# New orders for every engine of a LayerNorm, selective scan and int8 matmul kernel, from tables of place numbers

## The reference, cut to what matters

```python
def reference(x, A_log, D, x_proj_w, dt_proj_w, dt_proj_b, weight_q, weight_scale, bias):
    x = x + s6(layernorm(x), A_log, D, x_proj_w, dt_proj_w, dt_proj_b)
    x = x + quantized_ffn(layernorm(x), weight_q, weight_scale, bias)
    return x                                       # x is (8, 2048, 512) f32

def s6(x, ...):                                    # 512 features d, 16 states n
    xp = einsum('bld,ed->ble', x, x_proj_w)        # 64 ranks, 16 of B, 16 of C
    delta = softplus(xp[..., :64] @ dt_proj_w.T + dt_proj_b)
    h = exp(delta * -exp(A_log)) * h_before + delta * B * x    # for each row l in turn
    return sum over n of h * C + x * D

def quantized_ffn(x, ...):                         # 512 to 512
    x_scale = max(max(abs(x)), 1e-6) / 127.0       # of each row
    x_q = int8(clip(round(x / x_scale), -128, 127))
    return int32(x_q @ weight_q.T) * x_scale * weight_scale + bias
```

## Time and profile before

| | |
|---|---|
| median of 3 runs | 2763.84 us (2761.54 to 2764.33) |
| the profiled execution, first to last instruction | 2760.5 us |
| busy: PE, DVE, ACT, POOL | 2736.5, 2705.4, 2690.0, 2691.9 us |
| DVE: 2048 scans | 1828.9 + 584.8 us |
| POOL: 511 products by C | 2342.0 us |
| moved by DMA | 344.35 MB |

### The profile page before, as it was taken

The page is one execution under the profiler, slowest core; times in us unless marked ns, Lnnn a source line. Parts: engine busy times, 40 slices in busy tenths (PEclk is TensorE's granted clock), DMA queues, the critical chain, the costliest instruction groups (busy, mean ns, idle before and its releaser), DMA issues.

```text
span 2760.5 us, 59331 instructions
## 1 busy us (share of the span) xinstructions
PE 2736.5 (99%) x22612; PEld 2519.7 (91%) x22612; DVE 2705.4 (98%) x2801; ACT 2690.0 (97%) x4927; POOL 2691.9 (98%) x981
## 2 busy tenths in 40 slices
...
GB/s 198 100 101 139 123 116 148 107 124 133 118 142 117 120 142 123 116 143 112 124 131 116 145 112 117 149 112 127 137 118 124 127 117 149 111 113 154 99 133 54
DMA packets 271654, 344.35 MB, mean 125 GB/s; under 512 B 174917, under 2 KB 174917, under 8 KB 251018
## 3 DMA queue, kind: packets, MB, share of 16 engines
...
HBM read 253.60 MB, written 103.16 MB: 129 GB/s over the span
## 4 chain that ended last, share of the span: by engine, by line
PE 97%; DVE 1%; ACT 1%; issue 0%; DMA 0%; SPq 0%; DVEq 0%; POOL 0%; ACTq 0%
PE Y L855 32%; PE PB L830 23%; PE PB L833 21%; PE Y L851 4%; PE PM L962 4%; PE PM L921 4%; PE PM L902 4%; PE PM L892 2%; PE PM L930 2%; DVE A L994 1%; PE PM L909 0%; ACT A L669 0%; ACT DB L688 0%; PE PM L872 0%; PE PM L879 0%
## 5 line engine op out<-in xcount | busy, mean ns | idle before, releaser
L604 POOL TENSOR_TENSOR A<-A,CB 128x2048 f32<-128x2048 f32 x511 | 2342.0, 4747 | 42.4 <-ACT CAR L676 40.9
L994 DVE TENSOR_TENSOR_SCAN A<-A,CAR,PB 128x512 f32<-128x512 f32 x1536 | 1828.9, 1260 | 9.9 <-ACT A L669 4.6
L669 ACT ACTIVATE A<-DEL,an 128x512 f32<-128x512 f32 x2048 | 1332.5, 713 | 6.3 <-PE Y L855 5.8
L855 PE MATMUL Y<-idf,A 128*128 128x128 f32 x8192 | 1085.1, 273 | 0.0
L855 PEld LDWEIGHTS Y<-idf,A 128*128 128x128 f32 x8192 | 932.7, 141 | 6.5 <-issue 0.5
L688 ACT ACTIVATE DB<-XN,BC 128x512 f32<-128x512 f32 x1344 | 891.7, 711 | 3.6 <-DVE XN L1024 3.6
L833 PE MATMUL PB<-idf,DB 128*128 128x128 f32 x5376 | 764.1, 273 | 8.4 <-DVE A L994 7.0
L830 PEld LDWEIGHTS PB<-DG,XN 128*128 128x128 f32 x5632 | 685.9, 192 | 70.8 <-issue 48.3
L830 PE MATMUL PB<-DG,XN 128*128 128x128 f32 x5632 | 726.7, 276 | 2.5 <-DVE A L994 2.4
L833 PEld LDWEIGHTS PB<-idf,DB 128*128 128x128 f32 x5376 | 621.7, 141 | 66.3 <-issue 39.5
L994 DVE TENSOR_TENSOR_SCAN A<-A,PB 128x512 f32<-128x512 f32 x512 | 584.8, 1201 | 12.5 <-PE PB L833 7.4
...
## 6 DMA issues: line engine op xcount, KB each, us to landing
CB<-c_rows SPq DMA_DIRECT2D x128, 1024.0 KB, 4.8
DG<-b_diag SPq DMA_DIRECT2D x192, 256.0 KB, 5.0
X<-in_x SPq DMA_DIRECT2D x31, 1024.0 KB, 7.3
out<-X SPq DMA_DIRECT2D x31, 1024.0 KB, 5.2
out<-bias_rows POOLq DMA_DIRECT2D x31, 1024.0 KB, 8.8
out<-C POOLq DMA_DIRECT2D x31, 1024.0 KB, 12.7
...
b_diag<-BC SPq DMA_DIRECT2D x192, 2.0 KB, 5.4
```

The costliest lines, as they stand in the source:

```text
L604: gp.tensor_tensor(A[s % NA][:, :, :], A[s % NA][:, :, :], CB[:, s % (4 * NG), :].unsqueeze(1).broadcast_to([128, KB, L]), ALU.mult).then_ ...
L669: act.activation(A[s % NA][:, g, :], DEL[k % 2][:, g, :], ACT.Exp, scale=an[:, g, n:n + 1])\
L855: i = pe.matmul(Y[j][:, g * 128:(g + 1) * 128], A[s % NA][:, g, j * 128:(j + 1) * 128], idf[:, :], is_transpose=True, start=False, stop=(n ...
L994: dve.tensor_tensor_scan(A[s % NA][:, g, :], A[s % NA][:, g, :], PB[(4 * s + g) % NPB][:, :], init, ALU.mult, ALU.add).then_inc(s_scan, 1)
```

## The change

PERIOD goes from 1000 to 10000, and every number of PLACES, FIRST and LAST is replaced. No instruction is added to or removed from a chunk, and waits, tiles and sizes stay. The code below the tables is the same, 17 lines further down (L441 is L458 afterwards, L994 is L1011). Of the tables, two lines of PLACES:

```diff
-PERIOD = 1000
+PERIOD = 10000
 PLACES = {
...
-        "load_c": (107, 189, 717, 1001),
+        "load_c": (-1828, 3705, 4565, 6870),
...
-        "put_x": (1260,),
+        "put_x": (8967,),
```

More of the change, by code:

```diff
@@ L3 @@
 from contextlib import ExitStack
-PERIOD = 1000
+PERIOD = 10000
 PLACES = {
[L8 to L36, removed]
-        "load_c": (107, 189, 717, 1001),
-        "load_g": (35, 113, 310, 426, 1034, 1035),
-        "log0": (-1321,),
-        "put_last": (30000, 30001, 30002, 30003),
-        "put_x": (1260,),
[L42 to L60, removed]
[8 rows of a table removed]
[L69 to L80, removed]
@@ new lines @@
+        "act_b": (-2204, -2091, -2081, -2007, -1997, -1964, -1236, -1212, -1196, -470, -210, -161, -131, 203,
+        235, 278, 302, 464, 930, 1115, 1544, 2000, 2045, 2130, 2227, 2272, 2428, 2654, 2665, 3261, 3303, 4751,
+        5680, 5742, 5791, 5924, 6032, 6161, 6418, 6463, 6673, 6799),
+        "add_b": (19628,),
+        "add_c": (21943,),
+        "aggr0": (-11131,),
+        "amax": (14650,),
+        "ascale": (14042,),
+        "b_c": (-4324,),
+        "bc_out": (-5011,),
+        "bias_p": (200000, 200001, 200002, 200003),
@@ new lines @@
+        "idle": (200000, 200001, 200002, 200003),
+        "inv": (14968,),
+        "last_p": (200000, 200001),
+        "last_q": (200000, 200001, 200002, 200003),
+        "last_v": (200000, 200001),
+        "late": (200000, 200001, 200002, 200003),
+        "load": (-17500,),
+        "load_c": (-1828, 3705, 4565, 6870),
+        "load_g": (-4271, -3355, -1713, -192, 3547, 5496),
+        "log0": (-13308,),
+        "put_last": (200000, 200001, 200002, 200003),
+        "put_x": (8967,),
+        "q_mm": (18557, 18884, 20116, 20799),
@@ new lines @@
+        "q_t": (200000, 200001, 200002, 200003),
+        "qt_out": (17992, 19529, 20193, 23955),
+        "root": (14490,),
+        "rstd0": (-12916,),
+        "scale_a": (18084, 18731, 19205, 19848),
+        "scale_out": (200000, 200001, 200002, 200003),
+        "scale_p": (20893,),
+        "scales": (15617,),
+        "scan": (677, 897, 908, 931, 1340, 1345, 1345, 1345, 1345, 1345, 1353, 1353, 1548, 1608, 2429, 2586,
[4 rows of a table added]
+        "square": (13603, 13726, 14091, 14201),
+        "stats0": (-16595, -14243, -13892, -13758),
@@ new lines @@
+        "step": (15112,),
+        "store_c": (-2091,),
+        "store_g": (-4344,),
[8 rows of a table added]
+        "times_c": (252, 2574, 2845, 3650, 3931, 3936, 3942, 3981, 4386, 5182, 6947, 7062, 9064, 9717, 9807,
+        9949),
+        "turn": (17150,),
+        "var1": (14440,),
+        "warm": (200000, 200001, 200002, 200003, 200004, 200005, 200006, 200007, 200008, 200009, 200010,
+        200011),
+        "weights": (200000, 200001),
+        "x_p": (-5085, -5015, -4961, -4800),
+        "x_t": (-7595, -7130, -6858, -5430),
@@ L104 @@
[L104 to L125, removed]
@@ new lines @@
+        4074, 4082, 4164, 4301, 4827, 5313, 5348, 5399, 5662, 5683),
+        "add_b": (13976,),
+        "add_c": (22755,),
+        "aggr0": (-56395,),
+        "amax": (14678,),
+        "ascale": (14015,),
+        "b_c": (-58841,),
+        "bc_out": (-47619,),
+        "carry": (-361, 51, 421, 1952, 2030, 3180, 3468, 4394, 5109, 5368, 6433, 6555, 6971, 7088, 7908, 9360),
+        "centre": (15018, 15018, 15021, 16423),
+        "d_t": (-58762, -58091, -57284, -56741),
+        "decay": (-1680, -1458, -1424, -1406, -1404, -1404, -1404, -1404, -1404, -1394, -1391, -1304, -643,
[3 rows of a table added]
@@ new lines @@
+        "delta": (-46238, -38371, -37853, -36878),
+        "dl_t": (-50668, -49981, -43372, -41835),
+        "du": (-50897, -49054, -48113, -44153),
+        "gather": (11594, 12196, 12536, 12727),
+        "inv": (14875,),
+        "late": (-56500, -56400, 1000, 2000),
+        "load_c": (-56900, 3705, 4565, 6870),
+        "load_g": (-56800, -56700, -56600, -56300, 3547, 5496),
+        "log0": (-67199,),
+        "put_x": (14352,),
+        "q_mm": (18561, 18830, 19510, 20688),
+        "qt_out": (17846, 19083, 21458, 24188),
@@ new lines @@
+        "root": (14592,),
+        "rstd0": (-64776,),
+        "scale_a": (18302, 18701, 19418, 19751),
+        "scale_p": (21528,),
+        "scales": (15442,),
+        "scan": (699, 717, 717, 717, 717, 717, 721, 1043, 1043, 1059, 1101, 1188, 1724, 2210, 2371, 2442, 2582,
[4 rows of a table added]
+        "square": (12575, 13320, 13365, 13490),
+        "stats0": (-66507, -64549, -62297, -59886),
+        "step": (14395,),
+        "store_c": (-66375,),
+        "store_g": (-63242,),
[8 rows of a table added]
+        "times_c": (3601, 5384, 5547, 5683, 5829, 6218, 6767, 6942, 7433, 8752, 9636, 9832, 9844, 9844, 9984,
@@ L155 @@
+        10047),
+        "turn": (16687,),
+        "var1": (13568,),
+        "warm": (-50669, -50669, -1032, -1032, -1032, -1032, -1032, -1032, -1032, -1032, -1032, -1032),
+        "weights": (-659, 8151),
+        "x_p": (-63112, -59532, -59176, -59076),
+        "x_t": (-69956, -69193, -67385, -64745),
+        "xn": (-62645, -58697, -57917),
+        "xn_p": (-52454,),
+        "xp_out": (-54175,),
+        "xt_d": (-52727, -51805),
+        "xt_out": (-57532, -57272, -57272, -56808),
 }
@@ new lines @@
+        "aggr0": (-10553,),
+        "amax": (12118,),
+        "ascale": (12082,),
+        "b_c": (-4488,),
+        "bc_out": (-5434,),
+        "bias_p": (12332, 12336, 13115, 13540),
+        "carry": (-695, 434, 758, 1123, 2248, 2905, 3113, 4072, 5217, 5665, 6979, 7186, 7365, 7933, 8070, 8841),
+        "d_t": (-4062, -3929, -3802, -3548),
+        "decay": (-1977, -1790, -1490, -1146, -926, -811, -628, -619, -618, -614, -600, -153, 196, 233, 340,
[3 rows of a table added]
+        "delta": (-4588, -4478, -4209, -3682),
```

122 lines of the change are left out of this document (52 added, 70 removed), and 74 rows, old and new, of tables (FIRST, LAST, PLACES).

## The result

The changed kernel takes 2887.49 us (2886.3 to 2890.61, 4 runs) against 2763.45 (2761.54 to 2764.33, 4 runs): ratio 1.0452, 95% interval 1.0437 to 1.0466. That is 124 us more; forecast were 102 more, 2866 us, with a range to 2900.

What follows compares the result with a forecast made beforehand. PE, DVE, ACT and POOL in lockstep were taken as the bound, with DVE nearly full in three chunks of four. Steady chunks +98, opening +3 and end +1 gave +102, so 2866 us; range 2760 to 2900, likeliest case 2825 to 2900.

Steps and rivals of the forecast that it cites:

- L: Time from the end of the fourth gather until group 1 of CB has landed: 16.8 us, bounds 15 and 17.8.
- the share of `add_c`: What SP's queue loses to POOL's `add_c` transfer while group 1 is on its way: 4.7 us, added as 4.8.
- break-even in L: Landing time of group 1 behind the fourth gather up to which DVE's `scales` would not wait: 12.9 us.
- main term: 28 steady chunks, each 3.5 us longer because group 1 of CB lands late: +98 us.
- 36.2 and DVE's rest of a chunk: New pitch: gather to `scales` 36.2 us plus DVE's remaining 51.7, together 87.9, with small stalls 88.0, against 84.46.
- The wait on DVE: DVE idles 4.0 us in each chunk ahead of `scales` (L1064), released by POOL's `ascale` (L599).
- The clock, chance 0.10: Rival: PE's gap at `scales` lowers its clock in each chunk, +28 us on top, 2894 us; chance 0.10.
- The opening: Before chunk 1, DVE casts half the weights ahead of its first scan, which starts at 35.7, not 26.76: +3 us.
- Chunks 30, 31 and the end: Group 1 is late in chunk 30 too, less in chunk 31: +1 us, between -2 and +5.
- The other moves: Remaining new places, such as X's load, group 2 and `turn`: nothing while the late landing of group 1 holds the loop.
- faster: Rival: PE's and ACT's new lists remove DVE waits in chunks without CAR, giving 2756 us; chance 0.06.
- hidden: Rival: `add_c` moves mostly ahead of the gather, group 1 lands about 12 us behind it: 2761 to 2767; chance 0.12.

Runs made afterwards that it cites:

- cb1_ahead: Changed kernel with group 1 of CB issued ahead of the store of X, all else as changed: 2763.98 us, ratio 1.0006 to the kernel before.
- full_rows_scales_later: Changed kernel with 24 full-size idle PE transposes ahead of the wait for product n = 4 and DVE's `scales` three scans later: 2890.91 us, ratio 1.0462.
- x_behind: Changed kernel with the load of X put behind group 1 of CB, group 1 still behind the store of X: 2807.84 us, ratio 1.0166.
- thin_add_c: Changed kernel with `add_c` moving only one of its four row tiles, so the output is incomplete: 2776.43 us, ratio 1.0047.
- short_centre: Changed kernel with POOL's four centre operations of a chunk on 64 of 512 columns, quantized input mostly left out: 2846.37 us, ratio 1.0301.
- pe_full_rows: Changed kernel with 24 idle full-size PE transposes of zeros ahead of the wait for product n = 4, chunks 2 to 30: 2890.08 us, ratio 1.0462.
- scales_later: Changed kernel with DVE's `scales` three scans and a statistic later: 2912.90 us, ratio 1.0539.

## Why the prediction was right, and where it was not

**The place and the cause: right, and shown.** Group 1 of CB behind store, diagonal, X, diagonal; cb1_ahead takes it all back. L came to 16.45 against 16.8, and both of its parts were as worked out: without X it fell by 3.0 (forecast 2.9), without three quarters of `add_c` by 3.3 (4.8 x 0.75 = 3.6). The prediction works out 4.7 for the share of `add_c` and adds 4.8, a slip that is worth 3 us of the total. L also moves with the loop, as below (15.5 to 17.8 in variants with the same bytes), so that it fits within 0.4 is in part luck. The break-even in L was put at 12.9: at 10.1 nothing is lost, at 13.2 0.4 us a chunk.

**The size of the main term: 98 forecast, 121 measured.** The step that failed is "36.2 and DVE's rest of a chunk", with L taken as fixed. Gather to `scales` came to 36.41 and the rest to 52.38, against 36.2 and 51.7 with 0.1 for stalls. These look like two small misses, but the runs showed that this loop is not the one that sets the pitch: with DVE's wait at `scales` taken away in full_rows_scales_later nothing came back. What sets it is POOL. From the issue of `add_c` it is 19.7 us to the start of product n = 4, where POOL can start it after 14.4 if nothing is late (the issue and products n = 1 to 3, in cb1_ahead); then POOL has 69.0 us of work without a wait until the next `add_c`. 19.7 + 69.0 = 88.7, the distance of the issues of `add_c` (88.69 in chunks 4 to 27).

Two parts of one turn add up to it by construction, so the sum alone proves nothing. What it rests on is how the parts behave. The 69.0 is the same in the changed kernel, in x_behind (16.8 + 69.0 = 85.8), in thin_add_c (15.8 + 69.0 = 84.8) and in full_rows_scales_later, holds no wait, and fell to 67.5 in short_centre, where the pitch fell by as much. And the 19.7 doesn't follow the gather, which lies 3.1 us behind `add_c` in the changed kernel, 1.7 in full_rows_scales_later and 4.1 in short_centre: the group lands 19.5 to 19.6 us behind `add_c` in all of them, and L is what is left. Why it is just that time is argued, not shown: the transfers of both queues share the engines until the group has landed. No run moved `add_c` alone. Of the two times the prediction had one in hand: its 16.8 and "some 3 us" are 19.8 from `add_c` to the landing. It never added up POOL's work of a chunk, and looked only at who waits in one place.

**POOL's idle time was the term to take.** POOL's work is 69.0 + 14.4 = 83.4 us a chunk, 1.1 less than the pitch before. Its wait for group 1 is 19.7 - 14.4 = 5.3 (the profile shows 4.7 of it as idle, as its record of product n = 3 runs on for the rest). 28 x (5.3 - 1.1) = 118, against the 121 measured. This is worked out behind the result, from the traces of the changed kernel and cb1_ahead.

**The wait on DVE.** Forecast 4.0 us ahead of `scales`, released by POOL. Measured 4.3 us a chunk, but mostly earlier, ahead of the scan of n = 8, g = 2, behind PE's `th` of n = 4; at L1064 it is 15.9 us in all, in 15 waits. The prediction had named the chain over PE only as PE's and ACT's stop.

**The clock, chance 0.10.** It did fall, in 15 of the 28 steady chunks; in the one shown it was 0.66 over 5 us, a mixture of the two levels, after PE had been idle for 2.7. In the changed kernel it cost nothing that can be measured: with the clock at 1.00 in pe_full_rows the time is 2890.1 against 2887.5. PE's 44 us more of busy time lie in time that POOL's loop leaves free. The rival's mechanism was there in half of the chunks, and its price was nil as long as POOL did not wait for DVE; where it did, in scales_later, the clock was worth 22 us. The Trainium skill, "TensorE: Matmul & The Clock Gate", section "Why this matters for your kernels", warns of idle gaps between bursts of matmuls; the trace agrees that the clock can fall behind one, and shows that this need not cost.

**The opening: +3 forecast, +4.0 measured**, the first scan at 35.15 against 35.7. The cast there took 0.7 us, not 2.0, and the weights landed later than forecast. The timeline of DVE after:

```profile
34.53 0.69 DVE L992 CAST wqb<-C 128x1024 bf16<-128x1024 int32 x1 [4.72 <-DMA C<-in_wq]
35.15 2.32 DVE L1011 TENSOR_TENSOR_SCAN A<-A,PB 128x512 f32<-128x512 f32 x2
...
115.43 3.60 DVE L1011 TENSOR_TENSOR_SCAN A<-A,CAR,PB 128x512 f32<-128x512 f32 x3
```

**Chunks 30, 31 and the end: +1 forecast, +3.4 measured**, inside the -2 to +5 given.

**The other moves: nothing, as forecast.** Pitch 84.44 in cb1_ahead. The rivals "faster" and "hidden" missed because `add_c` runs inside L, as the argument against them had it.
